# Moving four of six stacking transfers from SyncE's queue to ScalarE's in a decoder's first stage

## The reference

```
def _L0_attn_ref(X, Wq, bq, Wk, bk, Wv, bv, Wo, bo):
    Q = (X @ Wq.T + bq).reshape(B, S, H, d_head) * scale
    K = (X @ Wk.T + bk).reshape(B, S, H, d_head) * scale
    V = (X @ Wv.T + bv).reshape(B, S, H, d_head)
    scores = jnp.einsum('bqhd,bkhd->bhqk', Q, K)
    scores = jnp.where(causal[None, None], scores, -jnp.inf)
    attn = jax.nn.softmax(scores.astype(jnp.float32), axis=-1).astype(X.dtype)
    out = jnp.einsum('bhqk,bkhd->bqhd', attn, V).reshape(B, S, D)
    return out @ Wo.T + bo
...
x = _layernorm(x + _L0_attn_ref(x, ...), axis=-1)
x = _layernorm(x + _L0_xattn_ref(x, ctx_2048, ctx_2048, L0_xattn_gamma), axis=-1)
...
```

## Time and profile before

| | |
|---|---|
| time, median of 3 runs | 1120.88 us (1119.94 to 1123.54) |
| the profiled execution | 1128.16 us |
| its span, first to last instruction | 1126.2 us |
| granted TensorE clock, mean | 0.941 |
| busy over the span: PE, DVE, ACT, POOL | 88%, 79%, 57%, 48% |
| stacking transfers | 96, 128 KB each, median 5.0 us from issue to landing |
| SyncE's queue (q1): bytes, share of 16 engines | 84.28 MB, 33.7% |
| ScalarE's queue (q10): bytes, share of 16 engines | 8.98 MB, 2.9% |

### The profile page before, as it was taken

The page is one execution under the profiler, slowest core; times in us unless marked ns, Lnnn a source line. Parts: engine busy times, 40 slices in busy tenths (PEclk is TensorE's granted clock), DMA queues, the critical chain, the costliest instruction groups (busy, mean ns, idle before and its releaser), DMA issues. The chain is left out here.

```text
span 1126.2 us, 25353 instructions
## 1 busy us (share of the span) xinstructions
PE 990.2 (88%) x8561; PEld 735.9 (65%) x8610; DVE 885.0 (79%) x2031; ACT 637.8 (57%) x1626; POOL 538.2 (48%) x983
## 2 busy tenths in 40 slices
PE   4669899983999966899999999999996999979996
PEld 3447667651555635788888888888884666546664
DVE  1448989933898967899999999999756899758885
ACT  2325555531798952555555555555452999944553
POOL 6337778873355543244444444444423465533322
PEclk8979999976899977999999999999998999989999
DMA  7888997733788530010000000003200666411111
GB/s 140 156 175 162 192 178 139 131 57 85 152 189 190 139 102 15 10 32 22 22 23 22 27 22 29 23 18 70 59 13 25 149 170 168 116 32 45 57 57 33
DMA packets 113631, 97.04 MB, mean 86 GB/s; under 512 B 16688, under 2 KB 106080, under 8 KB 113504
## 3 DMA queue, kind: packets, MB, share of 16 engines
q1 hardware_dynamic: 100032, 84.28, 33.7%
q10 hardware_dynamic: 11504, 8.98, 2.9%
q0 software_dynamic: 1968, 2.16, 1.2%
HBM read 64.97 MB, written 19.99 MB: 75 GB/s over the span
## 5 line engine op out<-in xcount | busy, mean ns | idle before, releaser
L402 DVE TENSOR_REDUCE ca_nm<-p_p 128x2 f32<-128x512 f32 x256 | 162.8, 678 | 19.0 <-PE p_p L300 17.7
L539 ACT ACTIVATE ca_pt<-p_p 128x512 f32<-128x512 f32 x256 | 142.7, 599 | 13.4 <-PE p_p L319 8.1
L300 PE MATMUL p_p<-ca_ks,ca_qs 96*128 96x256 bf16 x512 | 102.2, 284 | 19.6 <-DMA ca_ks<-k_parts 18.2
L1912 ACT ACTIVATE la_pq<-p_p,la_nm 128x128 f32<-128x128 f32 x256 | 90.1, 365 | 37.5 <-DVE la_nm L2015 37.5
L319 PE MATMUL p_p<-ca_qs,ca_ks 128*128 128x256 bf16 x512 | 101.4, 281 | 6.0 <-ACT ca_qs L531 2.4
L63 POOL TENSOR_TENSOR ca_pt<-la_lt,one 64x1024 f32<-64x1024 f32 x32 | 60.4, 1889 | 61.5 <-ACT la_lt L1891 60.3
L531 ACT ACTIVATE ca_qs<-p_p 32x1024 bf16<-32x1024 bf16 x64 | 65.0, 1016 | 43.0 <-PE p_p L309 41.5
L1896 ACT ACTIVATE la_qq<-p_p 128x512 f32<-128x512 f32 x32 | 19.1, 597 | 99.1 <-PE p_p L1728 99.1
L1066 DVE TENSOR_REDUCE sa_nm<-sa_p_s 128x4 f32<-128x512 f32 x64 | 43.7, 685 | 36.1 <-PE sa_p_s L926 35.6
L300 PEld LDWEIGHTS p_p<-ca_ks,ca_qs 96*128 96x128 bf16 x512 | 50.7, 101 | 32.5 <-DMA ca_ks<-k_parts 19.7
L1759 PE MATMUL p_p<-ca_pt,la_qq 128*128 128x128 f32 x512 | 70.4, 281 | 0.4 <-POOL ca_pt L63 0.3
(11 more groups left out here) (265 smaller groups left out, 2749.5 us busy)
## 6 DMA issues: line engine op xcount, KB each, us to landing
sa_qks<-sa_qkp SPq DMA_DIRECT2D x96, 128.0 KB, 5.0
ca_qs<-q_parts SPq DMA_DIRECT2D x32, 192.0 KB, 3.3
ca_ks<-k_parts SPq DMA_DIRECT2D x32, 192.0 KB, 3.8
ca_qs<-q_parts SPq DMA_DIRECT2D x32, 128.0 KB, 3.3
ca_ks<-k_parts SPq DMA_DIRECT2D x32, 128.0 KB, 3.8
ca_ct<-in_ctx_t SPq DMA_DIRECT2D x32, 128.0 KB, 3.7
ca_xr<-x_state SPq DMA_DIRECT2D x32, 128.0 KB, 2.1
x_state<-ca_xn SPq DMA_DIRECT2D x32, 128.0 KB, 2.1
```

Of the source, the lines that this page charges most:

```text
L300: last = pe.matmul(p_s[n % 3][:, qc, :], QS[b % 4][0:STACK, h, 128 * qc:128 * qc + 128], KS[b % 4][0:STACK, h, :], start=True, stop=True)
L402: dve.tensor_reduce(NM[b % 2][:, h, :], p_s[n % 3][:, :, :], AX.X, ALU.max, negate=True).then_inc(max_done, 1)
L539: act.activation(PT[g][:, j, :, :], p_e[n % 2][:, :, :], ACT.Exp, scale=SCALE).then_inc(exp_done, 1)
L1912: last = act.activation(PQ[g % 2][:, j, :], p_s[g % 2][:, j, :], ACT.Exp, bias=NM[b % 2][:, 4 * g + j:4 * g + j + 1], accum_out=SM[g % 2][ ...
```

## The change

`place`, which issues the transfers whose lowest part is `lowest`, becomes a function of the stage with the issuing engine as an argument. ScalarE's `middle(f)` now ends with the one transfer of the high part and the three of the middle part, behind three waits (the stack's buffer is free, the high part is written, the middle part is written). SyncE's `stacks(f)` waits for the buffer and the low part and issues two. Tiles, bytes and the semaphore that counts a stack's transfers stay.

```
+        def place(eng, f, lowest):
+
+            both = QKP[f % 2][:, :, :, :].rearrange("p n t c -> p (n t) c")
+            for t in range(NT):
+                q, k = Q_TERMS[t], 3 + K_TERMS[t]
+                if max(q, k - 3) == lowest:
+                    eng.dma_start(QKS[f % 3][HD * t:HD * t + HD, :, :, :], both[:, q:k + 1:k - q, :]).then_inc(stack_loaded[f % 3], 16)
...
             def stacks(f):
                 wait(sp, shifted_ready, G * (f - 2))
-                sp.wait_ge(qk_hi, f + 1)
-                place(f, 0)
-                sp.wait_ge(qk_mid, f + 1)
-                place(f, 1)
                 sp.wait_ge(qk_lo, f + 1)
-                place(f, 2)
+                place(sp, f, 2)
...
             def middle(f):
                 act.wait_ge(qk_rest, f + 1)
                 act.activation(QKP[f % 2][:, :, 1, :], QKR[:, :, :], ACT.Copy).then_inc(qk_mid, 1)
+                wait(act, shifted_ready, G * (f - 2))
+                act.wait_ge(qk_hi, f + 1)
+                place(act, f, 0)
+                act.wait_ge(qk_mid, f + 1)
+                place(act, f, 1)
```

More of the change, by code:

```diff
@@ L779, in load_more @@
                     load_cx(f + 2)
-            def place(f, lowest):
-                both = QKP[f % 2][:, :, :, :].rearrange("p n t c -> p (n t) c")
-                for t in range(NT):
-                    q, k = Q_TERMS[t], 3 + K_TERMS[t]
-                    if max(q, k - 3) == lowest:
-                        sp.dma_start(QKS[f % 3][HD * t:HD * t + HD, :, :, :], both[:, q:k + 1:k - q, :]).then_inc(stack_loaded[f % 3], 16)
             def stacks(f):
                 wait(sp, shifted_ready, G * (f - 2))
-                sp.wait_ge(qk_hi, f + 1)
-                place(f, 0)
-                sp.wait_ge(qk_mid, f + 1)
-                place(f, 1)
                 sp.wait_ge(qk_lo, f + 1)
-                place(f, 2)
+                place(sp, f, 2)
             def store_k(f):
```

## The result

| | before | after |
|---|---|---|
| median of 20 runs each, side by side | 1122.70 us (1118.42 to 1127.49) | 1125.57 us (1121.35 to 1132.95) |
| ratio to before, 95% interval | | 1.0031 (1.0016 to 1.0046) |
| the profiled execution | 1128.16 us | 1121.52 us |
| its span | 1126.2 us | 1119.5 us |

The changed kernel is slower by 0.31%, some 3.5 us. The forecast was 1121.0 us; 1125.6 lies inside the range of 1116 to 1127.5 and just above the likeliest case's own (1118 to 1124.5). Repeated later beside other kernels, the unaltered change gave 1.0052 (1.0027 to 1.0076).

A forecast was written before the change was run, and what follows sets the result against it. It took the first stage's steady steps to be bound by a GpSimd-ScalarE round, the early ones by transfers. Costs of 2.9 us and gains of 2.9 cancelled against the 1120.88 us median: 1121 us, range 1116 to 1127.5.

The forecast's parts named there:

- the likeliest case: First stage: costs and gains of the change cancel, about 1121 us, own range 1118 to 1124.5; chance 0.42.
- Price of the issues: ScalarE behind the middle part's copy: first issue hidden, three more at 0.65 us each; second exponential 2.1 us later per item.
- rival (d): ScalarE's issues held up behind a big load in step 6, costing at most 2 to 3 us; with rival (c) 0.18.
- What GpSimd passes on, 0.2 us an item: Steady steps: TensorE slips 1.2 us, but GpSimd starts only 0.2 us late, and only that adds up per item.
- rival (c): Steps 8 to 12: TensorE's 1.2 us slip adds up in full every item, 1127.2 us; with rival (d) 0.18.
- Steps 8 to 12 as five equal items, +1.1 us: Each of five steady items grows by GpSimd's 0.2 to 0.25 us, from 12.4 to 12.6 us, +1.1 in all.
- lost in full: +1.2: Step 3: TensorE waits for VectorE, which has no idle time, so the 1.17 us delay is not absorbed.
- The gains, -2.9 us: Early transfers: 2.0 from the raw weight load landing sooner, 0.4 from step 1's stack, 0.5 from step 7's.
- the stack at step 1: Start of step 1: TensorE's 0.4 us wait for the stack goes, six issues overlapping on two queues; -0.4.
- the third input: Start: third item's input issued 0.7 us sooner, first stacking transfer 1.3 us later; -1.0 to +1.5, taken as 0.
- Rival (b): First stage: transfers give back nothing, only ScalarE's issue time counts, +2.9, 1123.8 us; chance 0.20.
- GpSimd's 0.74 us wait stays: Steady steps: GpSimd's wait for ScalarE's middle part must stay 0.74 us; longer would mean the middle part's copy moved.

The follow-up runs named there:

- e8: The kernel before, with ScalarE issuing only the high part's transfer for every item and SyncE the other five; ratio to before 0.9990.
- e1: The change for items 0 to 4 only, SyncE issuing all six transfers for the others; 1122.56 us against 1121.58 before, ratio 1.0006.
- e5: The kernel before, with ScalarE issuing four transfers for item 15 alone, in step 13; ratio to before 1.0003.
- e2: The change from item 5 on only, SyncE issuing all six transfers for items 0 to 4; 1125.78 us, ratio to before 1.0037.
- e10: The change, unaltered, run once more beside other kernels; 1129.49 us against 1122.93 before, ratio 1.0052.
- e3: The change with ScalarE's four transfers issued later, behind its copy of the heads; 1133.87 us, ratio to before 1.0098.
- e6: The kernel before, with VectorE's two 16-element operations moved behind the division, SyncE issuing all six transfers; 1118.56 us, ratio to before 0.9970.
- e9: The kernel before, with ScalarE issuing four transfers for items 10 and 11 alone (steps 8 and 9); ratio to before 0.9999.
- e4_small_after: The change, with VectorE's two 16-element operations moved behind the division; 1121.65 us, ratio to before 0.9993.
- e11_loads_on_sync: e7_last_small with ScalarE's eight weight loads of step 1 and three of step 4 issued by SyncE; 1115.18 us, ratio to before 0.9924.
- e7_last_small: The kernel before, with ScalarE issuing four transfers for item 15 alone and VectorE's two 16-element operations moved behind the division; 1117.53 us, ratio 0.9958.

## Why the prediction was off where it was

- **Price of the issues.** Right in size. 2.77 us from the copy's start to the exponential (2.65), 2.14 us idle (2.1), 1.44 us wait of TensorE (1.39), the first issue hidden but for 0.23 us (e8). The waits came in steps 3, 7, 8, 11, 12 with 1.42 to 1.48 us, 0.55 in step 5 (0.5 forecast) and 0.83 in step 13. Step 7 was not forecast, and steps 9 and 10 do not have the wait: TensorE waits for VectorE ahead of it there. Of rival (d) a trace is left in step 6, where the four issues took 3.57 us instead of 2.61; the item is 14.17 us long, as before.
- **What GpSimd passes on, 0.2 us an item.** Half of it. The item became 12.81 us, not 12.6 (13.6 would have been rival (c)). VectorE's statistics came 0.96 us later in the item (from SyncE's `sa_xr`; 1.05 forecast) and GpSimd's step behind them started 0.13 us later (0.2 forecast). The missing 0.30 us is that step's own length, 0.58 instead of 0.28 us: it now lies beside VectorE's 0.69 us subtraction. The step that failed is "late by 0.2 us", and "that is the amount that counts": a delayed operation was given the duration of its old place. That VectorE's subtraction is what stretches it is read from the two lying side by side, not tested.
- **Steps 8 to 12 as five equal items, +1.1 us.** This is the mis-sized term that decides. With SyncE's issues the middle takes 132.6, 130.6, 132.5 and 132.0 us (before, e1, e5, e8), mean 131.9; with ScalarE's 137.4, 140.5 and 136.8 (the change, e2, e10), mean 138.2. That is +6.3 us, where steps 3 to 12 had 1.1 + 1.2 + 0.5 = 2.8. All of it lies in steps 8 to 12: 62.0 us with SyncE in each of these four traces, 69.6, 69.5 and 67.2 with ScalarE, on average +6.8 where +1.1 was forecast. Some 2.1 of it are five items longer by 0.42 us, the other 4.7 the items that went to 14.2 or 15.5 us. Steps 3 to 7 took 70.0 us on average with SyncE and 69.5 with ScalarE, where +1.8 at most was forecast; step 3, "lost in full: +1.2", became 0.4 us longer (12.80 to 12.93 us). I read TensorE's and VectorE's slip of 1.2 us as harmless because GpSimd did not wait for it; it brought VectorE's operations on top of GpSimd's. The trace of before had shown both kinds of item, in steps 4, 6 and 7 against 8 to 12, and I explained only the short ones.
- **The gains, -2.9 us.** Not shown, and not as large: e1_early has 1.0006, and its interval ends at 2.2 us of gain. The 5.6 us in place of 8.0 is what was forecast ("near 6") and yet weak evidence, since kernels with the old order show 6.1 to 9.0. That the stack's packets hold the load up was right (6.5 us to landing without them, e3); the failed step is that only the two low transfers would go on doing so once four stand "behind the load in the load's own queue": with them there the load took 7.3 to 8.9 us. Two terms had the wrong sign or none: the stack at step 1, -0.4, became +0.4 in three traces of four, and the third input, "I take 0", +0.6. The 1.73 us stack wait of step 7 was absent in one trace of the change and 1.6 us in the other. Rival (b), at 1123.8 us, had the gains right and the costs too low.
- **The tail.** Not in the sum. From step 13 on the kernels with ScalarE's issues take 53.0 to 53.6 us, those with SyncE's 55.1 to 58.8 (mean 57.2; before, e1, e6, e8, e9): -3.9 us, of which 2.4 lie in TensorE's busy time (31.3 against 28.9 us for the same products), which is clock; the rest was not taken apart. It hid more than half of the loss: +6.3 - 3.9 = +2.4 of the 3.5 us measured; the traces of the change being quick executions, the rest is not accounted for item by item. Whether the short tail belongs to the change stays open, since e5_last, with ScalarE's issues in step 13 alone, had 55.5.
- **GpSimd's 0.74 us wait stays**: right, as GpSimd's rows of steps 9 and 11 above show.
- The forecast's zero was thus several errors that cancelled in part: gains of 2.9 that did not come, against a tail of 3.9 that was not seen, and costs of 2.9 that are 6.3. That the time lies only 4.6 us from the forecast, and inside the range, owes much to luck.

## What to carry to other kernels

An issue on a computing engine costs its 0.65 us only if something behind it is on the path, but then it also shifts every engine against its neighbours: before costing a shift, look in the same trace for iterations of other lengths, and at which operations lie beside each other in them. A time taken once from a stretch that transfers decide is no baseline: with the same instructions up to step 3, e2_late took 86.8 us and e5_last 89.5, a difference as large as the gains that were read out of one trace. A cheap gain was not in the queues at all: two operations of 16 elements moved out from between a large GpSimd operation and the division that TensorE waits for gave 0.3%.

## What the runs showed of the hardware

- A VectorE operation on 128x16 elements takes 0.17 to 0.42 us alone and 0.97 to 1.15 us when it starts just behind a GpSimd operation on 128x512, ending 0.03 to 0.04 us after that one; when it starts later into such an operation it takes less (0.81 us in e4_small_after). The 128x256 normalisation goes from 0.40 to 1.36 us in the same way.
- Of the 19 items of steps 3 to 12 that took 15 us or more, over fourteen traces, 18 have a mean granted clock of 0.89, and one (step 3 of e11_loads_on_sync, behind a wait of 10.65 us) has 0.78; those of 14.17 to 14.23 us have 1.00. In the tail, in the five microseconds behind a wait of 1.64 or 1.86 us, the clock read 0.53 to 0.66 (before, e1, e5), a mean of its two levels of 1.2 and 2.4 GHz. A dip costs 1.4 us in an item (15.59 against 14.22) to 1.7 (14.48 against 12.81).
- Waits of TensorE of 1.6 to 2.0 us were followed by the low clock in some executions and not in others (1.99 us: 0.89 in the change, 1.00 in e9_two_steps; 1.70 to 1.72 us in step 4: 0.89 in before, e5, e8 and e9, 1.00 in e1; 1.64 us: 0.66 over the next 5 us in e5_last; 1.67 us: 1.00 in e7_last_small). This is a likely source of a part of the 7 to 13 us between executions of one kernel, though no run tested that by itself.
- SyncE and ScalarE are both held up when they issue the same small load behind two large ones: SyncE 5.96 us in its one trace, ScalarE 6.20 us in before and 4.40 to 5.04 in the twelve others.
